# A new hand-written order of all five instruction queues in the pair loop of a transformer decoder layer

## What is computed

```python
x = x + attn(layernorm(x))                       # one head of 256; three softmaxes, averaged:
#   causal scores; scores against keys averaged over groups of 4; the 64 largest raw scores of each row
x = x + cross(layernorm(x), ctx, mask)           # 16 heads of 64, scores = q k^T + mask
x = x + ffn(layernorm(x))                        # 256 -> 1024 -> 256, int8-like rounding, erf GELU
```

## Time and profile before

| | |
|---|---|
| Median of three runs | 1803.2 us |
| The profiled execution, its own time | 1802.63 us |
| Its span | 1800.8 us |
| Granted TensorE clock, mean | 0.975 of full speed; full in the pair loop |
| Busy PE / DVE / ACT / POOL | 88% / 84% / 58% / 57% |
| DMA | 39 GB/s on average |
| One round of the pair loop | 46.16 us |

### The profile page before, as it was taken

The page is one execution under the profiler, slowest core; times in us unless marked ns, Lnnn a source line. Parts: engine busy times, 40 slices in busy tenths (PEclk is TensorE's granted clock), DMA queues, the critical chain, the costliest instruction groups (busy, mean ns, idle before and its releaser), DMA issues. The chain is left out here.

```text
span 1800.8 us, 52126 instructions
## 1 busy us (share of the span) xinstructions
PE 1584.2 (88%) x16033; PEld 1398.1 (78%) x16052; DVE 1520.5 (84%) x6205; ACT 1044.1 (58%) x2181; POOL 1033.9 (57%) x1156
## 2 busy tenths in 40 slices
PE   4379999999999999999999999999999999848898
PEld 4368888888888888888888888888888888734465
DVE  4569989989888888888888888888988888539876
ACT  2145555566556555555666656555556655439875
POOL 0046666666766677667666676667666667622000
PEclk8699999999999999999999999999999999879999
DMA  5000000000000000000000000000000000032055
GB/s 169 27 9 24 23 21 26 26 25 23 26 26 26 26 26 26 26 26 22 22 26 26 26 26 26 26 26 26 26 26 26 26 26 21 14 119 81 31 169 176
DMA packets 77733, 71.02 MB, mean 39 GB/s; under 512 B 6272, under 2 KB 77184, under 8 KB 77696
## 3 DMA queue, kind: packets, MB, share of 16 engines
q1 hardware_dynamic: 74240, 68.17, 11.8%
q10 hardware_dynamic: 3456, 2.37, 0.5%
HBM read 45.36 MB, written 25.17 MB: 39 GB/s over the span
## 5 line engine op out<-in xcount | busy, mean ns | idle before, releaser
L588 POOL TENSOR_TENSOR exp_t<-exp_copy,exp_t 128x512 f16<-128x512 f32 x256 | 299.4, 1170 | 275.6 <-ACT exp_copy L944 275.6
L582 POOL TENSOR_TENSOR shifted<-scores,score_max 128x512 f32<-128x512 f32 x256 | 271.2, 1064 | 23.4 <-DVE score_max L1102 21.5
L1102 DVE CUSTOM_DVE_ANT_0 scores<-banks,mask 128x128 f32<-128x128 f32 x1024 | 232.6, 285 | 19.3 <-PE banks L779 11.4
L929 ACT ACTIVATE v_nat<-banks 128x512 f16<-128x512 f32 x128 | 77.3, 604 | 197.4 <-PE banks L108 197.4
L106 PE MATMUL banks<-ctx_t,cross_Wk 128*128 128x256 f32 x512 | 154.4, 302 | 34.3 <-DVE v_fold L1070 19.0
L574 POOL TENSOR_TENSOR v_nat<-kv_copy,v_nat 128x512 f16<-128x512 f32 x128 | 143.5, 1132 | 63.5 <-ACT kv_copy L932 63.5
L574 POOL TENSOR_TENSOR k_t<-kv_copy,k_t 128x512 f16<-128x512 f32 x128 | 149.2, 1175 | 34.5 <-ACT kv_copy L932 34.5
L788 PE MATMUL banks<-ident,shifted 128*128 128x128 f32 x1024 | 154.0, 278 | 7.6 <-POOL shifted L582 4.9
L942 ACT ACTIVATE exp_t<-banks 128x512 f16<-128x512 f32 x256 | 152.5, 596 | 8.6 <-PE banks L108 6.9
L944 ACT ACTIVATE exp_copy<-banks 128x512 f32<-128x512 f32 x256 | 155.5, 607 | 0.0
L932 ACT ACTIVATE kv_copy<-banks 128x512 f32<-128x512 f32 x256 | 153.0, 598 | 0.6 <-POOL k_t L574 0.6
(11 more groups left out here) (244 smaller groups left out, 5693.5 us busy)
## 6 DMA issues: line engine op xcount, KB each, us to landing
x_in<-in_x_dram SPq DMA_DIRECT2D x32, 256.0 KB, 2.7
ctx_in<-in_ctx_dram SPq DMA_DIRECT2D x32, 256.0 KB, 2.7
x_residual<-x SPq DMA_DIRECT2D x64, 128.0 KB, 1.7
x_normalised<-normed SPq DMA_DIRECT2D x32, 256.0 KB, 2.2
shared<-x_normalised SPq DMA_DIRECT2D x8, 1024.0 KB, 5.5
shared<-x_residual SPq DMA_DIRECT2D x16, 512.0 KB, 3.9
out_dram<-shared SPq DMA_DIRECT2D x16, 512.0 KB, 3.1
mask<-in_fside_Bx1xSxS_dram SPq DMA_DIRECT2D x64, 64.0 KB, 2.0
```

The source lines that it names most:

```text
L582: pool.tensor_tensor(shifted[:, q % 2], scores[:, q % 2], score_max[:, q % 2, :].unsqueeze(2).to_broadcast([P, QUAD, P]), ALU.subtract).th ...
L588: pool.tensor_tensor(exp_t[:, q % 2, LO], exp_copy[:, q % 2], exp_t[:, q % 2, HI], ALU.subtract).then_inc(exp_split, 1)
L929: op = act.activation(hilo(dst, *at)[HI], src, ACT.Copy)
L1102: op = dve.tensor_tensor_reduce(scores[:, q % 2, h, :], sc_bank(q)[:, tile(h)], mask[:, b, :], 1.0, NEG, ALU.add, ALU.max, score_max[:, q ...
```

## The change

The same calls are made with the same arguments; their order changes in all five lists. The job numbers of the two PE banks change with PE's order (K3 and X1 swap, the queries come in order with VV0 and VV2 between them, CTX comes last), and KV lists VV2 before VV1. On SyncE load_mask(1) moves up from behind store_x2(1) to behind load_mask(0).

On VectorE the end of the round becomes: top_round(7), lo(J_Q3), heads_lo(2), sparse, heads_lo(3), add_mask(2), add_mask(3), mix, second_residual(1), x2_statistics, lo(J_CTX), add_mask(4), largest_of_x2; and the next round begins add_mask(5), row_sums(0), divide(0), row_sums(1), lo(J_PT0), divide(1), statistics, add_mask(6), lo(J_PT1), normalise, row_sums(2), divide(2), heads_lo(0), lo(J_X). The diff, cut to the parts that are spoken of:

```diff
-(J_K0, J_K1, J_PT0, J_PT1, J_K2, J_X, J_AO, J_V0, J_G, J_V1, J_RAW, J_K3, J_X1, J_VV0,
- J_Q1, J_Q0, J_VV1, J_Q2, J_Q3, J_VV2, J_CTX, J_VV3) = range(22)
+(J_K0, J_K1, J_PT0, J_PT1, J_K2, J_X, J_AO, J_V0, J_G, J_V1, J_RAW, J_X1, J_K3, J_Q0,
+ J_Q1, J_Q2, J_VV0, J_Q3, J_VV2, J_VV1, J_VV3, J_CTX) = range(22)
-KV = (J_K0, J_K1, J_K2, J_K3, J_VV0, J_VV1, J_VV2, J_VV3)
+KV = (J_K0, J_K1, J_K2, J_K3, J_VV0, J_VV2, J_VV1, J_VV3)
...
@@ SyncE
                 if front:
                     load_mask(0, i)
+                    load_mask(1, i)
...
                     store_x2(1, i - 1)
-                if front:
-                    load_mask(1, i)
-                if back:
                     store_normed(i - 1)
...
@@ GpSimd
                 if back:
                     exp_lo(1, i - 1)
+                    exp_lo(2, i - 1)
                 if front:
                     lo(J_K0, i)
+                if back:
+                    keep_x1(i - 1)
                 if ahead:
                     reciprocal_deviation(i + 1, moments_x, moments, var_eps, eps_x, rstd, rstd_x)
                 if back:
-                    exp_lo(2, i - 1)
-                    keep_x1(i - 1)
+                    exp_lo(3, i - 1)
                     shift(5, i - 1)
-                    exp_lo(3, i - 1)
                     shift(6, i - 1)
                     exp_lo(4, i - 1)
                 if front:
                     reciprocal_deviation(i, moments_x1, moments1, var_eps1, eps_x1, rstd1, rstd_x1)
                 if back:
-                    shift(7, i - 1)
+                    exp_lo(5, i - 1)
                 if front:
                     lo(J_K1, i)
                     lo(J_K2, i)
                 if back:
-                    exp_lo(5, i - 1)
+                    shift(7, i - 1)
...
                 if front:
                     lo(J_VV0, i)
-                if ahead:
-                    add_output_bias(i + 1)
-                if front:
+                    shift(1, i)
+                    exp_lo(0, i)
+                    lo(J_VV2, i)
+                    shift(2, i)
                     lo(J_VV1, i)
-                    shift(0, i)
-                    exp_lo(0, i)
-                    shift(1, i)
+                    shift(3, i)
                 if back:
                     x2_deviation(i - 1)
                 if front:
-                    shift(2, i)
-                    shift(3, i)
-                    lo(J_VV2, i)
                     lo(J_VV3, i)
                     shift(4, i)
...
@@ TensorE
+                if back:
+                    exp_transpose(3, i - 1)
+                    weigh(0, i - 1)
                 if front:
                     keys(0, i)
                     keys(1, i)
-                if back:
-                    weigh(0, i - 1)
-                if front:
                     probs_transpose(0, i)
                 if back:
+                    weigh(1, i - 1)
                     scores(3, i - 1)
-                    exp_transpose(3, i - 1)
+                    weigh(2, i - 1)
+                    heads_transpose(0, i - 1)
                 if front:
                     probs_transpose(1, i)
                     keys(2, i)
...
@@ ScalarE
+                if back:
+                    exponential(2, i - 1)
                 if front:
                     hi(J_K0, i)
+                    hi(J_PT0, i)
                     hi(J_K1, i)
-                    hi(J_PT0, i)
                     hi(J_PT1, i)
                 if back:
-                    exponential(2, i - 1)
+                    heads_hi(0, i - 1)
+                    exponential(3, i - 1)
...
@@ VectorE
                 if back:
                     add_mask(5, i - 1)
+                    row_sums(0, i - 1)
+                    divide(0, i - 1)
+                    row_sums(1, i - 1)
+                if front:
+                    lo(J_PT0, i)
+                if back:
+                    divide(1, i - 1)
                 if ahead:
                     statistics(i + 1, x_in, stats, stats_x, moments, moments_x)
                 if back:
-                    row_sums(0, i - 1)
-                if front:
-                    lo(J_PT0, i)
-                if back:
                     add_mask(6, i - 1)
-                    divide(0, i - 1)
                 if front:
                     lo(J_PT1, i)
                 if ahead:
                     normalise(i + 1, x_in, moments, rstd, rstd_x, xn, xn_ready)
                 if back:
-                    row_sums(1, i - 1)
-                    divide(1, i - 1)
...
```

More of the change, by code:

```diff
@@ L843, in body @@
                 if back:
[L844 to L845 removed]
+                    weigh(3, i - 1)
                 if ahead:
@@ L1238, in body @@
                 if back:
-                    row_sums(1, i - 1)
-                    divide(1, i - 1)
+                    row_sums(2, i - 1)
+                    divide(2, i - 1)
+                    heads_lo(0, i - 1)
                 if ahead:
@@ L1244, in body @@
                     first_residual(i)
+                if back:
+                    add_mask(7, i - 1)
+                if ahead:
+                    lo(J_V0, i + 1)
+                if back:
+                    row_sums(3, i - 1)
+                if front:
                     statistics(i, x1, stats1, stats_x1, moments1, moments_x1)
                 if back:
-                    row_sums(2, i - 1)
-                    divide(2, i - 1)
-                    heads_lo(0, i - 1)
+                    divide(3, i - 1)
                 if ahead:
-                    lo(J_V0, i + 1)
                     lo(J_G, i + 1)
                 if back:
-                    add_mask(7, i - 1)
+                    row_sums(4, i - 1)
                 if front:
@@ L1277, in body @@
                 if ahead:
+                    top_round(i + 1, 2)
+                    window_and_compressed(i + 1)
+                if front:
+                    lo(J_Q1, i)
+                    lo(J_Q0, i)
+                if ahead:
                     top_round(i + 1, 3)
                 if back:
-                    row_sums(5, i - 1)
+                    divide(5, i - 1)
                 if ahead:
@@ L1283, in body @@
                 if back:
-                    divide(5, i - 1)
-                if ahead:
-                    window_and_compressed(i + 1)
+                    second_residual(0, i - 1)
                 if front:
-                    lo(J_Q0, i)
-                    lo(J_Q1, i)
+                    add_mask(0, i)
                 if ahead:
                     top_round(i + 1, 5)
-                if back:
-                    second_residual(0, i - 1)
-                    row_sums(6, i - 1)
+                if front:
+                    lo(J_Q2, i)
                 if ahead:
@@ L1297, in body @@
                 if back:
+                    row_sums(6, i - 1)
+                if front:
+                    add_mask(1, i)
+                if back:
+                    divide(6, i - 1)
                     row_sums(7, i - 1)
-                    divide(6, i - 1)
+                    divide(7, i - 1)
                 if ahead:
                     top_round(i + 1, 7)
-                    sparse(i + 1)
-                if back:
-                    divide(7, i - 1)
-                if front:
-                    add_mask(0, i)
-                if back:
-                    heads_lo(2, i - 1)
-                    heads_lo(3, i - 1)
-                if front:
-                    add_mask(1, i)
-                    lo(J_Q2, i)
-                if ahead:
-                    mix(i + 1)
                 if front:
@@ L1317, in body @@
                 if back:
-                    second_residual(1, i - 1)
-                    x2_statistics(i - 1)
+                    heads_lo(2, i - 1)
+                if ahead:
+                    sparse(i + 1)
+                if back:
+                    heads_lo(3, i - 1)
                 if front:
@@ L1322, in body @@
                     add_mask(3, i)
+                if ahead:
+                    mix(i + 1)
+                if back:
+                    second_residual(1, i - 1)
+                    x2_statistics(i - 1)
                 if ahead:
```

101 lines of the change are left out of this document (46 added, 55 removed).

## The result

The changed kernel takes 1820.0 us (median of four runs, 1815.45 to 1827.64) against 1802.8 us for the kernel before, measured beside it. The ratio is 1.010, with a 95% interval of 1.0082 to 1.0118: slower by 1%. The forecast was 1790, with a range up to 1820, so both the sign and the likeliest case were wrong; the measured median lies at the very end of the range. The profiled execution took 1815.45 us, the fastest of the four; its span is 1813.6 us, 12.8 over the one before. The spread of the runs, 12 us, is itself new: the four runs of the kernel before stayed within 3 us. Only one execution was profiled, but the mean granted clock of all four is on record: 0.965 and 0.966 at 1815.45 and 1816.68 us, 0.963 at 1823.32, 0.961 at 1827.64. So the slower executions are those with the lower clock.

The account below looks back on a forecast made before the run. DVE's in-order list was taken to bound the 46.16 us round, with PE near full. Gaining 1.25 and losing 0.79 gave 45.70, 13.8 us over thirty rounds: 1790 us, own range 1780 to 1798, 8-in-10 range 1756 to 1820.

Parts of the forecast that it names:

- E: The end of x2_statistics on DVE, where segment one begins; 820.24 in the kernel before.
- X: The start of lo(J_X) on DVE, where segment one ends; 833.86 in the kernel before.
- segment one: DVE from end of x2_statistics to start of lo(J_X), joining two rounds: forecast 12.37 instead of 13.62, a gain of 1.25.
- Segment two: The rest of the round, from lo(J_X) to the next end of x2_statistics: 32.54 us before, forecast loss 0.79.
- The filling of DVE's wait: Row_sums and divide of 0 and 1 and lo(J_PT0) moved into DVE's 1.4 us wait for the x load.
- the POOL slack: POOL's queue reached x's 1/deviation 1.30 us after the load's chain; the slack that the change can take.
- largest_of_x2's new wait: DVE waits for ACT until 3.12 us after x2_statistics ends; inside the wait for the load, so costs nothing.
- The forecast of 0.46 for the order: Net gain per round: 1.25 in segment one less 0.79 lost in segment two, giving a round of 45.70.
- my sum keeps the blocks as they were: DVE instructions held by a running POOL instruction, 0.91 us a block, were assumed unchanged; called the largest unknown.
- a further one at x1's normalise: Slower rival: POOL blocks x1's normalise twice, adding 0.91 to segment two; round 46.61, time 1817; chance 0.28.
- All rivals: x1's normalise blocked twice (1817, chance 0.28); one block fewer in mix (1762, 0.25); no difference (1802, 0.11).
- inside the time PE waits for normalise anyway: PE's wait at the round's start for the bank of K0, under 1 us, was taken as covered by its normalise wait.

Follow-up runs that it names:

- e9: Changed kernel with GpSimd's exp_lo(3) waiting for x's normalise (e1), and load_mask(1) back behind store_x2(1): 1757.7 us.
- e2: Changed kernel with keep_x1 back behind x's 1/deviation, as before the change: 1812.5 us, ratio 1.005.
- e8: Changed kernel with e1's wait, load_x issued a round earlier, e4's last round, and GpSimd's lo(J_VV1) waiting for mix: 1707.0 us, ratio 0.947.
- e11: Kernel before, own order, load_x issued a round earlier, GpSimd's exp_lo(2) waiting for x's normalise and exp_lo(0) for mix: 1718.8 us, ratio 0.953.
- e1: Changed kernel with one wait added: GpSimd starts exp_lo(3) only when VectorE's normalise of x is done: 1759.3 us, ratio 0.976.
- e5: Kernel before the change, with GpSimd's exp_lo(2) starting only when normalise of x is done: 1772.8 us, ratio 0.984.
- e4: Changed kernel with round 32 alone in the order of before on TensorE, ScalarE, VectorE and GpSimd: 1816.9 us, ratio 1.007.
- e13: Changed kernel with GpSimd's lo(J_VV1) starting only when mix is done, nothing done about x's normalise: 1790.1 us, ratio 0.993.
- e10: e1 with VectorE's statistics of x back directly behind add_mask(5), as before the change: 1865.7 us, ratio 1.036.
- e12: Changed kernel with SyncE's load_mask(0) in front of load_x, so the load is issued about 0.7 us later: 1867.4 us, ratio 1.036.

## Why the prediction was wrong, point by point

- **The sum for the round is near the length of 16 rounds in 29, in part by luck.** Read in the short round: E = 728.66 + 0.25 = 728.91, X = 741.15, so segment one is 12.24 (forecast 12.37; in it E to statistics 6.96, forecast 6.93). Segment two, from X to 774.74, is 33.59 (forecast 33.33). Together 45.83 (forecast 45.70). The filling of DVE's wait, the POOL slack, largest_of_x2's new wait (1.8, cost nothing: it lies inside the chain of the load) and load_mask(1) (e9) were as argued. But the sum kept x's pair at 1.85, and in the short round it takes 1.57. Where it takes 1.83, in e2, the round is 46.13, 0.43 over the forecast: segment one 12.52 in the mean, segment two 33.60. The forecast of 0.46 for the order stands against 0.03 with x's blocks as they were (e2), 0.36 in the short rounds, 0.42 (e8 against e11) and 0.67 (e1 against e5), and in the last two x1's pair has lost its block as well. So what the order gives hangs on the blocks, which the text took for a matter apart.
- **The step that failed is "my sum keeps the blocks as they were".** The text called them the largest unknown, gave a block 0.91, and then put a further one at x1's normalise with a chance of 0.28. It came at x's normalise. Before the change this pair was blocked as well, by an exp_lo and by keep_x1 behind it, the shortest of these instructions (0.67); the change puts keep_x1 in front of 1/deviation and a shift in its place. So the pair of 1.85 became 1.57, blocked once, in 16 rounds and 2.28 to 2.45, blocked twice, in 13, and the 13 are 0.94 longer than the 16. The walk did not set the times of exponential(3) on ScalarE and of 1/deviation against each other; they are 0.1 us apart. At x1's normalise DVE came first (746.25 against GpSimd's 746.50 in the short round), as the text's own argument against that rival had it, and the pair grew only from 1.45 to 1.59. The text's sign of being wrong, an xn pair over 2 us, is met in the 13 rounds.
- **It isn't one state but a draw in every round.** All rivals gave one length for all rounds. The trace of before shows the draw's input: its waits for the load are not all alike, 1.43 in one round, up to 1.7 in the next ones. There the variation was harmless, because POOL's queue, ending 1.30 later, hid it. The change took that 1.30 as slack, and with it the cover that kept the load's variation off normalise. That is the gain and the loss in one step.
- **TensorE's clock was no term.** Had all 29 rounds been short, the loop would have gained 10.4 us; the 13 blocked ones cost 13 x 0.94 = 12.2, and the fall of the clock in seven of them 7 x 0.95 = 6.7, which makes the net loss of 8.5. Before, TensorE's longest wait in a round was 1.4 us; it became 2.4. The text used this wait only as cover for another one ("inside the time PE waits for normalise anyway") and gave its length no price.
- **The last two rounds were left out of the sum.** 7.3 us of the 12.8 are theirs, 4.5 to 6 of them by the order if the seven other kernels are taken (e4): an order in which another pair's calls fill each wait has nothing to fill them with when the back half is alone. e4 shows that it is the order of round 32. With this the whole distance is told: from 13.8 gained in the forecast to 12.8 lost in the profiled execution are 26.6 us, of which the blocks make 12.2, the last two rounds 7.3, the clock in the loop 6.7 and the sum of the round 3.4, less 3.0 for the stretches ahead of the loop and behind it.
- The rival's time, 1817, is near the measured 1820, but that is luck: its place and its single length are not what happened, and the time was made up by the blocks at x's normalise, the clock and the last two rounds.
- By the Trainium skill ("SBUF — State Buffer", Terms) the port pair is held for the full instruction and the loser stops altogether. The runs agree with it in size: a pair of 0.74 becomes 1.57 behind one GpSimd instruction, 1.83 behind 0.63 and 1.15, 2.28 behind 1.15 and 1.09. What the trace adds is that in the middle round GpSimd's next instruction goes ahead of the second xn instruction, too (785.29 against 785.41), so that two VectorE instructions in a row are each held by one of GpSimd's.

What stays open: which of the rounds with a TensorE wait of 2.4 us lose the clock. In the changed kernel it was seven of 13, in e4 13 of 17 and in e13 11 of 19, all with 2.4; in e2 five of 29 with 1.6 to 2.0, in e10 all with 2.0 to 2.3, in e12 all with 2.7 to 3.1; with waits up to 1.5 none did. So the length of the wait isn't all that decides. That the wait lowers the clock is argued from this company, and what else is needed was not tested. Nor was the new order of round 31 tried by itself.

## What to carry to other kernels

When two engines share a port, an order of queues is only as good as the instruction that happens to be ready on the other engine at that moment. If a critical VectorE instruction of a kind that is blocked (here xn from SBUF to SBUF, and mix's with two SBUF operands) follows on a GpSimd result, let GpSimd wait for it before it goes on: in e1 a wait of 1.0 us on an engine with slack bought 1.3 us against the short round. A slack that an order removes may be the cover of something that varies, so look at the spread of a wait before removing what hides it, and read single rounds, not means, when a loop gets slower. Cost the first and last rounds on their own.

## What was not expected of the hardware

- A difference of 0.1 us or less in a load's landing decided 0.9 us of a round, and with the clock 1.9, with a sharp edge: 2.74 us short, 2.75 us long, in 29 of 29 rounds.
- VectorE's time behind the ports is booked as busy. DVE busy fell from 41.5 to 38.2 us a round with no instruction removed, so 3.4 us of an engine that seemed 90% full were waits.
- The granted clock fell to 0.50 for 3.4 us behind a wait of TensorE of 2.4 us, in seven of 13 such rounds, on an engine that is busy 42.4 of 46.7 us in the others; it cost 0.95 us a round.
